# Layer norm of a graph network: the normalising step on VectorE, block by block, in place of GpSimd

## The reference

```python
def _layernorm(x, axis=-1, eps=1e-05):
    m = jnp.mean(x, axis=axis, keepdims=True)
    v = jnp.var(x, axis=axis, keepdims=True)
    return (x - m) / jnp.sqrt(v + eps)
...
# L0: h = relu(adj @ (f1 * (adj @ (x @ W1)))); out = adj @ (f2 * (adj @ (h @ W2)))
# L1: concat([x, adj @ x]) @ weight
# L2: messages = x @ W_msg + b_msg; q, k from messages
#     gates = sigmoid(q @ k.T / scale + gate_bias) * adj * adj
#     u = relu(concat([x, gates @ messages]) @ W_upd + b_upd)
#     out = (u - mean(u)) * rsqrt(var(u) + 1e-5) * ln_gamma + ln_beta
# L3: twice swish((adj @ x) @ W + b)
x = _layernorm(x + _L0_gnn_ref(...), axis=-1)
x = _layernorm(x + _L1_gnn_ref(...), axis=-1)
x = _layernorm(x + _L2_gnn_ref(...), axis=-1)
x = _layernorm(x + _L3_gnn_ref(...), axis=-1)
```

## Time and profile before

| | us |
|---|---|
| median of 3 runs | 1895.87 |
| lowest, highest | 1895.03, 1899.65 |
| span of the profiled execution | 1896.7 |
| VectorE busy | 1494.3 |
| TensorE busy | 1683.2 |
| ScalarE busy | 1007.3 |
| GpSimd busy | 471.2 |

### The profile page before, as it was taken

One profiled execution on the slowest core, in us unless ns is written; L12 is line 12 of the kernel. 1 busy time (PEld: TensorE's weight loads), 2 busy tenths in 40 slices (PEclk: granted clock), 3 DMA queues, 4 the chain that ended last, 5 costly groups with the idle time before them and its releaser, 6 DMA issues.

```text
span 1896.7 us, 18699 instructions
## 1 busy us (share of the span) xinstructions
PE 1683.2 (89%) x7618; PEld 776.0 (41%) x7618; DVE 1494.3 (79%) x1231; ACT 1007.3 (53%) x709; POOL 471.2 (25%) x187
## 2 busy tenths in 40 slices
PE   7999999999999899898978786786786879999986
PEld 4444444444444444444433342242232434444432
DVE  6874565537556974788999999999999997654997
ACT  5764455446445543655646654554554756553753
POOL 1000000000000210112475656756756140000022
PEclk9999999999999999999989988888888999999999
DMA  9986776647766756666723433333333679764983
GB/s 374 391 315 232 258 312 248 240 176 285 268 243 230 280 206 239 246 246 240 266 89 133 149 118 111 118 126 111 112 132 111 240 252 353 286 232 171 351 304 139
DMA packets 59206, 423.64 MB, mean 223 GB/s; under 512 B 6800, under 2 KB 6960, under 8 KB 8304
## 3 DMA queue, kind: packets, MB, share of 16 engines
q1 hardware_dynamic: 57888, 417.88, 59.8%
q0 software_dynamic: 1088, 4.49, 0.7%
q10 hardware_dynamic: 144, 0.07, 0.0%
HBM read 420.32 MB, written 2.10 MB: 223 GB/s over the span
## 4 chain that ended last, share of the span: by engine, by line
PE 51%; DVE 34%; issue 9%; ACT 2%; POOL 1%; DMA 1%; SPq 0%; POOLq 0%; DVEq 0%; ACTq 0%
PE acc L502 32%; PE spare L502 15%; DVE gates L867 10%; DVE a_lo L851 9%; DVE a_lo L843 7%; ACT a_hi L677 2%; DVE bn L773 2%; PE rows L415 1%; PE rows L408 1%; DMA a_ring<-adj_dram 1%; DVE stats L784 1%; POOL x_rows L918 1%; DVE stats L787 1%; PE rows L421 1%; DVE moments L776 1%
## 5 line engine op out<-in xcount | busy, mean ns | idle before, releaser
L843 DVE SCALAR_TENSOR_TENSOR a_lo<-a_ring,a_hi 128x2048 f16<-128x2048 f32 x332 | 777.3, 2365 | 308.2 <-ACT a_hi L677 307.8
L677 ACT ACTIVATE a_hi<-a_ring 128x2048 f16<-128x2048 f32 x332 | 630.0, 1907 | 419.1 <-PE spare L502 275.1
L502 PE MATMUL acc<-a_hi,y_hi 128*128 128x512 f16 x1584 | 488.1, 390 | 157.9 <-DVE a_lo L851 121.4
L502 PE MATMUL acc<-a_hi,y_lo 128*128 128x512 f16 x1584 | 489.8, 391 | 0.0
L502 PE MATMUL acc<-a_lo,y_hi 128*128 128x512 f16 x1584 | 489.5, 391 | 0.0
L957 POOL TENSOR_TENSOR a_ring<-a_ring 128x1024 f32<-128x1024 f32 x112 | 312.1, 2813 | 97.2 <-DMA a_ring<-adj_dram 97.2
L909 POOL TENSOR_TENSOR val<-val,moments 128x1024 f32<-128x1024 f32 x19 | 51.2, 2694 | 1027.6 <-DVE moments L776 1027.6
L502 PEld LDWEIGHTS acc<-a_hi,y_hi 128*128 128x128 f16 x1584 | 150.2, 99 | 367.6 <-DVE a_lo L851 153.5
L685 ACT ACTIVATE a_hi<-gates 128x1024 f16<-128x1024 f32 x128 | 135.2, 1056 | 246.1 <-DVE gates L867 246.1
L851 DVE TENSOR_TENSOR a_lo<-gates,a_hi 128x1024 f16<-128x1024 f32 x128 | 263.5, 2058 | 0.0
L867 DVE SCALAR_TENSOR_TENSOR gates<-gates,a_ring 128x1024 f32<-128x1024 f32 x128 | 258.6, 2021 | 0.0
(11 more groups left out here) (111 smaller groups left out, 979.3 us busy)
## 6 DMA issues: line engine op xcount, KB each, us to landing
a_ring<-adj_dram SPq DMA_DIRECT2D x396, 1024.0 KB, 5.1
x_T<-xt_dram SPq DMA_DIRECT2D x4, 512.0 KB, 8.1
x_rows<-x_dram POOLq DMA_DIRECT2D x1, 2048.0 KB, 10.6
out_dram<-x_rows POOLq DMA_DIRECT2D x3, 512.0 KB, 4.6
out_dram<-x_rows SPq DMA_DIRECT2D x2, 256.0 KB, 2.0
w<-W_dram POOLq DMA_DIRECT2D x2, 64.0 KB, 5.4
wcat<-Wcat_dram POOLq DMA_DIRECT2D x1, 128.0 KB, 7.0
wupd<-W_upd_dram POOLq DMA_DIRECT2D x1, 128.0 KB, 7.6
```

Source lines behind the costliest of these rows:

```text
L502: mm = pe.matmul(sums[:, h * BANK:(h + 1) * BANK], blk(y[:, y_pass % 2, :], j), slot(a, st)[:, s, h * BANK:(h + 1) * BANK], start=(begins ...
L677: act.activation(slot(a_hi, st), loaded(st), ACT.Copy, scale=2.0 ** A_EXP).then_inc(s_ahi, 1)
L843: dve.scalar_tensor_tensor(out=slot(a_lo, st).rearrange("p s c -> p (s c)"), in0=loaded(st).rearrange("p s c -> p (s c)"), scalar=2.0 ** A ...
```

## The change

VectorE applies the layer norms, in place of GpSimd. The plain norm is one TENSOR_SCALAR per block of 128x128, `(val - mean) * rstd`, with mean and rstd as per-partition scalars. The affine norm is two SCALAR_TENSOR_TENSOR per block: `(val - mean) * gain`, then `* rstd + offset`. `centre`, `normalise` and `affine` leave GpSimd's queue, which keeps the squares and the stores of pass 8; nothing else is reordered. The eight BN and eleven `stats` instructions stay as they are, and so do TensorE, ScalarE and SyncE but for the semaphore `affine_done`, in whose place `residual` waits for `ln_done`.

```diff
-    "affine": {6: 2},
...
             def residual(p, k):
                 if p == GATED:
-                    dve.wait_ge(s_aff, nth("affine", p, k, 1))
+                    dve.wait_ge(s_ln, nth("ln", p, k, 0))
...
+            def normalise_blocks(blocks, dst, n):
+
+                dve.wait_ge(s_newton, 3 * NEWTON * n)
+                for b in blocks:
+                    op = dve.tensor_scalar(dst(b), val[:, b, :], moments[:, b, 0:1], stats[:, 1, b:b + 1], ALU.subtract,
+                                           ALU.mult)
+                op.then_inc(s_ln, 1)
...
+            def normalise_affine(p, k):
+
+                n = nth("ln", p, k, 0)
+                dve.wait_ge(s_newton, 3 * NEWTON * n)
+                for b in range(CB):
+                    dve.scalar_tensor_tensor(out=xn[:, b, :], in0=val[:, b, :], scalar=moments[:, b, 0:1], in1=gam[:, :],
+                                             op0=ALU.subtract, op1=ALU.mult).then_inc(s_scaled, 1)
+                for b in range(CB):
+                    dve.wait_ge(s_scaled, CB * (nth("resid", p, k) - 1) + b + 1)
+                    op = dve.scalar_tensor_tensor(out=xn[:, b, :], in0=xn[:, b, :], scalar=stats[:, 1, b:b + 1],
+                                                  in1=bet[:, :], op0=ALU.mult, op1=ALU.add)
+                op.then_inc(s_ln, 1)
...
-                4: {0: [take_over], 1: [values, ln_moments(0, s_val, "val"), ln_rstd(0)], 5: [y_low]},
-                5: {0: [take_over], 1: [values], 2: [ln_moments(0, s_val, "val"), ln_rstd(0)],
+                4: {0: [take_over], 1: [values, ln_moments(0, s_val, "val"), ln_rstd(0), normalise(0)], 5: [y_low]},
+                5: {0: [take_over], 1: [values], 2: [ln_moments(0, s_val, "val"), ln_rstd(0), normalise(0)],
...
-                6: {5: [values], 8: [ln_moments(0, s_nl, "nonlin")], 10: [ln_rstd(0)], 15: [residual],
-                    17: [ln_moments(1, s_res, "resid")], 20: [ln_rstd(1)], 23: [y_low]},
+                6: {5: [values], 8: [ln_moments(0, s_nl, "nonlin")], 10: [ln_rstd(0)], 12: [normalise_affine],
+                    15: [residual], 17: [ln_moments(1, s_res, "resid")], 20: [ln_rstd(1)], 21: [normalise(1)],
+                    23: [y_low]},
...
-                8: {0: [take_over], 2: [swish], 4: [residual], 5: [ln_moments(0, s_res, "resid")], 6: [ln_rstd(0)]},
-                LAST_GATED: {2: [values], 4: [ln_moments(0, s_nl, "nonlin")], 5: [ln_rstd(0)], 8: [residual],
-                    10: [ln_moments(1, s_res, "resid")], 11: [ln_rstd(1)], 14: [y_low]},
+                8: {0: [take_over], 2: [swish], 4: [residual], 5: [ln_moments(0, s_res, "resid")], 6: [ln_rstd(0), normalise(0)]},
+                LAST_GATED: {2: [values], 4: [ln_moments(0, s_nl, "nonlin")], 5: [ln_rstd(0)], 6: [normalise_affine],
+                    8: [residual], 10: [ln_moments(1, s_res, "resid")], 11: [ln_rstd(1), normalise(1)], 14: [y_low]},
...
             swish_half(0)
             moments_half(0)
             swish_half(1)
             rstd_half(0)
+            normalise_half(0)
             moments_half(1)
             rstd_half(1)
+            normalise_half(1)
...
-            stages = {
-                4: {3: [centre(0), normalise(0)]},
-                5: {3: [centre(0), normalise(0)]},
-                6: {8: [centre(0)], 12: [normalise(0)], 13: [affine], 18: [centre(1)], 21: [normalise(1)]},
-                8: {5: [centre(0), normalise(0), store]},
-                LAST_GATED: {5: [centre(0)], 6: [normalise(0), affine], 11: [centre(1)], 12: [normalise(1)]},
-            }
+            stages = {8: {6: [store]}}
```

More of the change, by code:

```diff
@@ L812, in ln_rstd, with normalise, go @@
                 return go
+            def normalise_blocks(blocks, dst, n):
[4 more added lines that the diff above has]
+                op.then_inc(s_ln, 1)
+            def normalise(run):
+                def go(p, k):
+                    normalise_blocks(range(CB), lambda b: normalised(p, k, run)[:, b, :], nth("ln", p, k, run))
+                return go
+            def normalise_affine(p, k):
[9 more added lines that the diff above has]
+                op.then_inc(s_ln, 1)
             def qk_low(run, hi, lo, exp):
@@ L889, in rstd_half, with normalise_half @@
                 rstd_of(range(h * HB, (h + 1) * HB), CB * last("ln", 0) + (h + 1) * HB, last("ln", h + 1))
+            def normalise_half(h):
+                first = ORDER[PASSES][NC - 1] * CB
+                normalise_blocks(range(h * HB, (h + 1) * HB), lambda b: x_rows[:, first + b, :], last("ln", h + 1))
             swish_half(0)
@@ L904, in _ @@
                                pattern=[[-1, P]], channel_multiplier=1).then_inc(s_id, 1)
-            def centre(run):
-                def go(p, k):
-                    pool.wait_ge(s_moments, CB * nth("ln", p, k, run))
-                    pool.tensor_tensor(val[:, :, :], val[:, :, :], over_features(moments[:, :, 0]),
-                                       ALU.subtract).then_inc(s_cen, 1)
-                return go
-            def normalise(run):
-                def go(p, k):
-                    n = nth("ln", p, k, run)
-                    pool.wait_ge(s_cen, n)
-                    pool.wait_ge(s_newton, 3 * NEWTON * n)
-                    pool.tensor_tensor(normalised(p, k, run), val[:, :, :], over_features(stats[:, 1, :]),
-                                       ALU.mult).then_inc(s_ln, 1)
-                return go
             def store(p, k):
@@ L958, in _ @@
             epilogue(stages, at, THE_END)
-            for h in range(HALVES):
-                blocks, first = slice(h * HB, (h + 1) * HB), ORDER[PASSES][NC - 1] * CB + h * HB
-                pool.wait_ge(s_moments, CB * last("ln", 0) + (h + 1) * HB)
-                mean, rstd = [v.unsqueeze(2).to_broadcast([P, HB, F])
-                              for v in (moments[:, blocks, 0], stats[:, 1, blocks])]
-                pool.tensor_tensor(half(val, h), half(val, h), mean, ALU.subtract).then_inc(s_cen, 1)
-                pool.wait_ge(s_cen, last("ln", h + 1))
-                pool.wait_ge(s_newton, 3 * NEWTON * last("ln", h + 1))
-                pool.tensor_tensor(x_rows[:, first:first + HB, :], half(val, h), rstd,
-                                   ALU.mult).then_inc(s_ln, 1)
 def kernel(**inputs):
```

9 lines of the change are left out of this document (2 added, 7 removed).

## The result

| | before | after |
|---|---|---|
| median of 4 runs, us | 1896.8 | 1848.3 |
| lowest, highest | 1895.0, 1899.7 | 1847.4, 1849.1 |
| ratio | | 0.974 (95%: 0.973 to 0.976) |
| span of the profiled execution | 1896.7 | 1847.1 |

The table has the runs made together with those of the changed kernel, with a fourth run of the kernel before. So the spans differ by 49.6 us and the medians by 48.5.

A forecast was written before the change was run, and what follows sets the result against it. VectorE, waiting out GpSimd's instructions, was taken to bound the gated pass, TensorE the rest. Gated pass -22, pass 4 +4, pass 5 -3, pass 7 -3.5, pass 8 -2.5 made -27 us: median 1869 us, range 1852 to 1886.

The forecast's parts named there:

- What bounds the kernel: VectorE sets the pace in the gated pass, losing 1.7 us to each GpSimd instruction beside it; elsewhere TensorE is the bound.
- Taken away and added in the gated pass: Per chunk 11.2 us of VectorE time go and 24 small instructions add 6.0: 15.5 us net for three chunks.
- dearer rival: Small instructions cost 0.29 us each, 192 over the whole kernel, 7.5 us more: 1876; chance 0.17.
- The squares: Gated pass: nothing to two squares hidden per chunk, 0 to 3.4 us; one taken, 5 us for three chunks.
- Pass 4: Eight small instructions delay the split TensorE waits for by 2.0 us; its second wait goes: together +4, up to +7.
- pass 5: Normalised rows and `a_lo` come sooner, 1 us three times: -3, to -8 if the clock holds.
- Pass 7, head: VectorE loses 9.5 us of blocked instructions and waiting, and gains 24 small ones, 6.0: -3.5.
- Pass 8: Per chunk the blocked `stats` and TensorE's second wait go, eight small instructions come: -0.9, three times, -2.5.
- end: Behind pass 8: small instructions +1.0, a shorter `stats` instruction 0.7, GpSimd's step replaced -0.2; the sum is nothing.
- The slower rival: Gated pass: small instructions wait out square after square, bursts of 18 us starve TensorE: 1924, or 1897; chance 0.06.
- lower prices hold: Small instructions cost 0.14 us each and two squares are hidden: about 1850; chance 0.06.

The follow-up runs named there:

- experiment 7: The kernel before, norms still on GpSimd, but with all squares on ScalarE: 1779.1 us, ratio 0.938.
- experiment 4: The changed kernel, with GpSimd waiting in the gated pass where its norm instructions stood, without their work: 1860.9 us, ratio 0.981.
- Experiment 3: The changed kernel plus a stand-in, one GpSimd instruction over 128x1024 per chunk of passes 4 and 5 at the old subtraction's place: 1866.2 us.

## Why the prediction was off

*What bounds the kernel* held. A GpSimd instruction beside VectorE's costs VectorE nearly its whole length (1.7 us of 1.9), and in the gated pass VectorE sets the time. The runs with fewer squares show how much there was: 165 us of VectorE's time in the changed kernel (171.0 less 5.9), none of which the change was meant to take.

*Taken away and added in the gated pass* held: 36.4 us by experiment 7 where the prices made 37.0, and 0.26 against 0.25 for a small instruction. The dearer rival at 0.29 is ruled out. The Trainium skill's formula, page VectorE: DVE Perf Modes, section on the TRN2 errata, gave 0.29 as an estimate; the rows show 0.26 from one start to the next. One instruction by itself is under way for 0.34, so they overlap.

*The squares* was the first step that failed. It said that one square per chunk would hide beside BN_STATS and its neighbours, and bounded it at two. Excess fell by 18 us where 5 were taken; 10 was the upper bound. The mechanism, squares running where GpSimd used to wait, was right (13.6 us by experiment 4), its size off by more than two; the second half of it, squares held up while VectorE runs on at 1.22, I had not thought of. BN_STATS did keep its 1.63 us beside squares (seven of its rows in the changed kernel have one beside them), as the Trainium skill's page SBUF — State Buffer, section Who interferes with whom, has it.

New idle time, 8 us, goes the other way and was not in the sum. VectorE waits twice for a square, 3.7 us in all:

```profile
1181.12 2.83 DVE L893 SCALAR_TENSOR_TENSOR gates<-gates,a_ring 128x1024 f32<-128x1024 f32 x1 [1.86 <-POOL a_ring L960]
```

and near the start of the pass three times for ScalarE and TensorE, 4.6 us in all.

*Pass 4* and *pass 5* were the steps that failed most, by 4.3 and 12.2 us, and for one reason. The forecast read the earlier trace rows from the end of the Newton steps on. The `stats` instruction of 1.77 us stood just ahead of it, and it is the very thing that the earlier trace rows show for pass 7, where I did price it (1.87 for 0.17), as I did in pass 8. I did not carry the term over. It is 1.6 us in each of eight chunks, seven of them ahead of the gated pass. Experiment 3 puts the collision back: it costs 4.8 us in pass 4 and 10.1 in pass 5, and with it in place the forecast's +4 and -3 come out as +4.5 and -5.1. In pass 5 TensorE's wait became so much shorter that the clock stayed up in every chunk; the forecast named that (to -8, if the clock holds) and took the end without it. Of the three parts of the 3.79 us per chunk one (0.88) was in the sum, at 1; one (the clock) in the bound alone; and one (the `stats` instruction) nowhere.

*Pass 7, head*: -4.9 against -3.5; the cause of the other 1.4 stays open. *Pass 8* and the *end*: -2.5, as forecast.

*The slower rival* had its mechanism the wrong way round. It let squares cut up the rows of small instructions; the rows of eight took 2.18 even where a square lay beside them, and the engine held up was GpSimd. The reason given against it, a mostly empty stock, was not what decided there: in each of the three chunks a square had begun by the second row of eight, and the row ran on.

*The range* was too narrow: all lower prices at once came to 1846 in the text, and it stopped at 1852, with the result between them. The rival *lower prices hold* was put at 1850, but its own terms, 192 times 0.11 and 5 us for the second squares, make 26 us less than 1869, or 1843. That the result lies near is no sign for it: the small instructions cost 0.26 and not 0.14.

## What to carry to other kernels

Where two engines exclude each other, list every instruction of the waiting one that lies beside one of the other, in every stage: here an instruction of 0.17 us lost 1.6, about as much as one of 1.21 (1.7). Then follow the loss one engine further, as TensorE's longer wait cost it another 1.4 us per chunk at its lower clock. And when a trace shows that one engine's work is paid for by another, ask for all of that work and not only for the part that a change touches: here the norms were worth 48 us, and the squares left beside them another 110.

## What the runs showed of the hardware that I had not expected

GpSimd can be the one that is held up, and for long. Single squares of 17.0, 18.9, 17.0, 19.3 and 17.0 us stand in the gated pass of the changed kernel, where an undisturbed one takes 1.9. VectorE's instructions start every 1.14 us there and last 1.22, so each begins before the one ahead has ended, and the square ends when VectorE comes to BN_STATS or waits. In the changed kernel they begin in or just behind a row of small instructions, and with wide ones in their place the longest is 8.3. But the rows are not needed: the kernel with the stand-in has one of 16.1 us that begins at 1049.4 among unit instructions alone, and the two in the kernel where GpSimd waits (17.3 and 14.8) begin over 8 us behind the nearest row. In other stretches with the same two unit instructions, the two engines take turns, 2.91 us for each of VectorE's. What decides between the two patterns no run here settles.

TensorE's clock moved after short waits, and not each time. Before, in pass 5, the granted clock was 0.50 (1.2 GHz) behind a wait of 3.16 us. After, it stayed at 1.00 (2.4 GHz) when eight transposes stood in the middle of the gap and 1.11 us of waiting was left. With the stand-in, 1.37 us of waiting, eight transposes and 1.11 us more were followed by 0.50 in two chunks and by 1.00 in the third. In pass 4 after, a wait of 2.50 in place of 1.92 was followed by 0.51 some 1.3 us later, for about 3.4 us, in chunk 2, while behind the same wait in chunk 3 (773.99) the clock stayed at 1.00.
